# Routing with fewer TensorE transposes: every fourth tile's rows of the second half turned by VectorE and DMA, the last fold by halves of slots, two stores by halves

## The chip, the cores and the metric

The kernel runs on one core of a Trainium2 chip. A core has five engines that run side by side: TensorE (PE; its weight loads are shown apart as PEld), VectorE (DVE), ScalarE (ACT), GpSimd (POOL) and SyncE (SP), which here issues transfers; 16 DMA engines carry them. The metric is the time of one launch in microseconds (us). Before the change it was 578.08 us, the median of three runs (577.79 to 578.09). In code P is 128, the partitions.

## The reference, cut to what matters

Four batches of 2048 tokens of 256 numbers go through a layer of linear attention and then a soft mixture of experts; all numbers are float32. The change touches the second part alone, where N is 64 tiles of 128 tokens here (the 16 experts with 16 slots give 256 columns):

```python
x = layernorm(x + attention(x))                       # not touched
xn = layernorm(x) * gamma + beta
logits = einsum('bnd,des->bnes', l2norm(xn) * scale, l2norm(mu))
dispatch = softmax(logits, axis=tokens)               # over the tokens of a batch
combine = softmax(logits, axis=(experts, slots))
slot_in = einsum('bnd,bnes->besd', xn, dispatch)      # the "fold"
h = gelu(einsum('besd,edh->besh', slot_in, w1) + b1)
slot_out = einsum('besh,ehd->besd', h, w2) + b2
out = layernorm(x + einsum('besd,bnes->bnd', slot_out, combine))   # the "mix"
```

## The kernel before, in words

The second part has three stages. **Routing** goes over 64 tiles of 128 tokens, four batches of TB = 16 tiles; four tiles (GT) are a group, and there are 16 groups (GROUPS), group k with its tokens in buffer q = k % 4. For each group GpSimd adds beta to the scaled tokens (`add_beta`), TensorE turns the rows by eight transposes, four tiles by two halves of the 256 numbers (`turn_xn`, L257), ScalarE rounds the turned tokens from the accumulator banks to xnT_hi (`round_xnT`, L264), and VectorE subtracts to get the rest xnT_lo (`split_xnT`, L269). For each tile TensorE then makes the logits with six matmuls (L1736 to L1738, hi and lo parts), ScalarE the exponentials e_tok (L1634), and TensorE folds the tokens with them: two float32 matmuls, one for each half of the 256 slots (L1748; a float32 matmul appears in the trace as two). Logits run two tiles ahead of the fold (`LEAD`). VectorE turns each tile's exponentials in blocks of 32x32 (L1853), SyncE moves the blocks to their place with four transfers for each group (`exchange_e`, L1477), and from group 4 on it spills the tokens of a group to memory (`spill_x1`, L1487). VectorE also scales the tokens of group k+3 (L222), and GpSimd inverts the norms (L249) and makes ET_lo (L1542).

**Slots**: VectorE normalises the folded slots (`normalise_slots`, L1907 and L1909), TensorE turns them (L1776), multiplies by w1 and w2 (L1793, L1805) with ScalarE's gelu between, VectorE adds the bias in 16 pieces (L1944), and TensorE turns the outputs back with 16 transposes (L1814), four for each batch; ScalarE copies them out of the banks (L1694), VectorE makes three rests (L1953).

**Mix**: for each group TensorE multiplies (L1841 for groups 0 to 3, L1837 to L1839 for the rest), VectorE adds the tokens (L1963) and takes statistics (L1976), GpSimd and ScalarE help (L1588, L1702) and ScalarE normalises (L1709). SyncE reloads spilled tokens (L1501) and stores each finished group of 512 KB (L1520). The last group goes out in two halves, one issued by ScalarE (L1722) and one by SyncE (L1522).

The order on each engine is written out by hand, and semaphores tie the engines together. What waits where, around the change: the logits of a group's first tile wait for `xnT_split`; the exponentials of a tile wait for the turn of the tile four before (`e_turned`); a group's first turn of exponentials waits until the transfers of the group two before have landed (`e_moved`); SyncE issues strictly in its order.

Of the kernel before, what the change touches and what calls it, by code (L numbers as in the profile page):

```python
# [21 lines left out]
P = 128  # L22
# [7 lines left out]
def build(nc, x, xT, W1q, b1q, W2qT_b, W1k, b1k, W2kT_b, W1v, b1v, W2v, b2v, ln_w, ln_b,  # L30
# [21 lines left out]
    with top:  # L52
# [207 lines left out]

        def round_xnT(act, k, q):
            act.wait_ge(xnT_done, k + 1)
            for kb in range(KB):
                nc.scalar.copy(xnT_hi[q % 2][:, kb, :], xnT_ps[kb][:, :]).then_inc(xnT_rounded, 1)  # L264

        def split_xnT(dve, k, q, halves=range(KB)):
            for kb in halves:
                dve.wait_ge(xnT_rounded, KB * k + kb + 1)
                nc.vector.tensor_tensor(xnT_lo[q % 2][:, kb, :], xnT_ps[kb][:, :],  # L269
                                        xnT_hi[q % 2][:, kb, :].bitcast(F32), ALU.subtract).then_inc(xnT_split, 1)  # L270


        with ExitStack() as attn:
# [1077 lines left out]
        with ExitStack() as moe:  # L1351
# [3 lines left out]
            def msem(name):  # L1355
                return sem(name, moe)
# [9 lines left out]
            xnT_hi.append(msb("xnT_hi1", [P, KB, GTOK], F32R))  # L1366
            xnT_lo.append(msb("xnT_lo1", [P, KB, GTOK], F32R))
            e_tok = msb("e_tok", [P, 4, ES])
            e_turn = [msb(f"e_turn{i}", [P, FOUR, SB, GT, QUAD]) for i in range(2)]
            SPLIT = (1, 2, 3)  # L1370
            FIRST = GB * SPLIT[0]
# [90 lines left out]
            last_stored = [msem(f"last_stored{pair}") for pair in range(2)]  # L1462

            block = moe.enter_context(nc.Block())

            @block.sync
            def _(sp):
                for kb in range(KB):
                    sp.dma_start(w1_sb[:, kb, :, :], w1[:, kb * P:(kb + 1) * P, :].rearrange("e p h -> p e h")
                                 ).then_inc(w1_loaded, 16)  # L1470

                def exchange_e(g):

                    sp.wait_ge(e_turned, GT * g + 2 * GT)
                    for j in range(FOUR):
                        quad = slice(QUAD * j, QUAD * j + QUAD)
                        sp.dma_start(ET_all[:, g, :, quad],  # L1477
                                     e_turn[g % 2][quad, :, :, :, :].rearrange("r f s t c -> r (f s t c)")
                                     ).then_inc(e_moved[g % 2], 16)

                def spill_x1(g):

                    sp.wait_ge(tok_scaled, GT * g)
                    n = g - FIRST
                    if n > 1:
                        sp.wait_ge(x1_spilled[n % 2], 16 * (n // 2))
# [25 lines left out]
                for g in range(FIRST, AGAIN):  # L1512
                    reload_x1(g)
                for k in range(LAST):
                    if k + AGAIN in SPLIT_GROUPS:
                        reload_x1(k + AGAIN)
                    sp.wait_ge(y_normed, GT * k + GT)
                    if k >= GB:
                        sp.wait_ge(stored[k % GB], 16 * (k // GB))
                    sp.dma_start(out_t[:, GT * k:GT * k + GT, :], y[k]).then_inc(stored[k % GB], 16)  # L1520
# [3 lines left out]
                for pair in range(2):  # L1524
                    sp.wait_ge(last_stored[pair], 16)
                for q in range(GB):
                    sp.wait_ge(stored[q], 16 * (B - 1 if q == LAST % GB else B))

            @block.gpsimd
            def _(pool):  # L1530
# [14 lines left out]
                def route(b, last):  # L1545
                    for q in range(GB):
                        if not (last and q == GB - 1):
                            if b == 0 and q == 1:
                                invert_o(pool, GROUPS - 1, 1)
                            if b > 0 or q > 0:  # L1550
                                invert_norms(pool, GB * b + q + 1, (q + 1) % GB, minus_half[:, :])
                        if not (last and q >= GB - 3):
                            add_beta(pool, GB * b + q + 3, (q + 3) % GB)
                        if GB * b + q - 2 in SPLIT_GROUPS and not (last and q == GB - 1):
# [73 lines left out]
            def _(act):  # L1628
# [97 lines left out]
            def _(pe):  # L1726
                def logits(b, t):
                    q = t // GT % GB
                    toks = slice((t % GT) * P, (t % GT + 1) * P)
                    if t % GT == 0:  # L1730
                        pe.wait_ge(xnT_split, KB * (GB * b + t // GT + 1))
                    pe.wait_ge(e_ready, TB * b + t + 1)
                    ps = log_ps[t % 2][:, 0:ES]
                    for kb in range(KB):
# [6 lines left out]
                def fold(b, t):  # L1741
# [3 lines left out]
                    if t == 0 and b > 1:  # L1745
                        pe.wait_ge(slot_inT_ready, SB * b)
                    for s in range(SB):
                        last = nc.tensor.matmul(fold_ps(b)[s][:, 0:D + 1], e_tok[:, t % 4, s * P:(s + 1) * P],  # L1748
                                                xn[q][:, t % GT, :], start=(t == 0), stop=(t == TB - 1))
                        if b == B - 1 and t == TB - 1 and s == 0:  # L1750
                            last.then_inc(half_folded, 1)
                    last.then_inc(tile_folded, 1)

                def lead(b, t, last):
                    logits(b, t)
                    k, q = GB * b + t // GT + 1, (t // GT + 1) % GB
                    if t % GT == 1 and not (last and q == 0):
                        turn_xn(pe, k, q)

                def route(b, last):  # L1760
                    for t in range(TB):
                        if t < TB - 1 and not (last and t + LEAD >= TB):
                            lead(b, t + LEAD, last)
                        fold(b, t)
                        if t == 1 and b > 0:
                            turn_slots(b - 1)
# [33 lines left out]
                for half in range(2):  # L1800
                    pe.wait_ge(hs_ready, half + 1)
                    for db in range(KB):
# [3 lines left out]
                                                    w2_sb[:, r, db * P:(db + 1) * P], hs[:, r, :],  # L1806
                                                    start=True, stop=True)
                        last.then_inc(soT_done, 1)
                for n in range(B):
                    pe.wait_ge(soT_ready, 3 * B + n + 1)  # L1810
                    for s in range(SB):
                        for db in range(KB):
                            at = s * D + db * P
                            last = nc.tensor.transpose(so_ps[n][:, at:at + P],  # L1814
                                                       soT[:, db, n, s * P:(s + 1) * P], ident[:, :])
                    last.then_inc(so_done, 1)
# [29 lines left out]
            def _(dve):  # L1846
# [10 lines left out]
                def route(b, last):  # L1857
                    a, p = GROUPS - 1, 1
                    for t in range(TB):
# [28 lines left out]
                        if b == 1 and t == 10:  # L1888
                            shift_z(dve, a, p)
                        if t % GT == 1 and not (last and q == GB - 1) and not (b == 0 and q == 0):  # L1890
                            split_xnT(dve, k + 1, (q + 1) % GB)
# [158 lines left out]
```

## Time and profile before

| what | value |
|---|---|
| median of 3 runs | 578.08 us |
| the profiled execution's own time | 578.1 us |
| its span | 576.4 us |
| PE busy | 564.3 us (98% of the span) |
| DVE, ACT, POOL busy | 84%, 71%, 74% |
| granted TensorE clock, mean | 0.995 of full speed |
| DMA | 59.66 MB, 166932 packets, of them 139854 under 512 B |

The profiled execution lies 1.7 us above its span and agrees with the median. Busy time of an engine is counted from the records of its instructions; for PE the ends of matmuls are modelled, so that records overlap, and what a matmul costs in a full queue is the distance to the start of the next one. In the second part, routing runs from 394 to 509 us of the span, the slots to 520, the mix to 568, and the rest until 576.4 is the end of the last groups and their stores.

### The profile page before, as it was taken

Reading aid. Unit: us, or ns where it says so; the run is one execution under the profiler, and the core shown is the slowest. Engines: PE = TensorE matmul, PEld = TensorE weight load, DVE = VectorE, ACT = ScalarE, POOL = GpSimd, SP = SyncE. Lnnn points to the kernel's source line nnn. Section 1 sums busy time; section 2 is a strip of 40 time slices with the busy share of each in tenths; the row PEclk is TensorE's granted clock in tenths of the full one; section 3 lists DMA queues with packets and bytes.
Section 4 is the critical chain, followed back from the end, with each engine's and each line's share of the span. In section 5 each row is a group of like instructions: output and inputs, shape, how many; then the busy total and the mean of one; then the engine's idle time right before and its main releaser. Section 6 shows DMA issues by size and latency. Waiting matters only on the chain. (4 is left out here: it accounts for less than half of the span.)

```text
span 576.4 us, 12092 instructions
## 1 busy us (share of the span) xinstructions
PE 564.3 (98%) x3892; PEld 525.8 (91%) x3892; DVE 486.1 (84%) x1037; ACT 406.7 (71%) x870; POOL 425.7 (74%) x437
## 2 busy tenths in 40 slices
PE   8999999999999999999999999999999999999994
PEld 7999989999899999999999999998999999988994
DVE  6579889799898889988889889988989777557996
ACT  4775666676767667667576766677679988754886
POOL 0779879788797887977979779795667777643664
PEclk9999999999999999999999999999999999999997
DMA  8424134042240422413224133023777777784986
GB/s 219 102 75 110 24 88 91 21 111 34 77 109 6 104 31 78 109 15 94 38 72 109 18 91 73 3 38 74 148 151 146 146 147 145 130 136 136 327 295 220
DMA packets 166932, 59.66 MB, mean 104 GB/s; under 512 B 139854, under 2 KB 159724, under 8 KB 166892
## 3 DMA queue, kind: packets, MB, share of 16 engines
q1 hardware_dynamic: 166608, 58.89, 43.9%
q8 instruction: 21, 0.34, 0.2%
q10 hardware_dynamic: 284, 0.27, 0.1%
q14 instruction: 19, 0.16, 0.1%
HBM read 27.68 MB, written 14.68 MB: 74 GB/s over the span
## 5 line engine op out<-in xcount | busy, mean ns | idle before, releaser
L529 POOL TENSOR_TENSOR h_lo<-xn_all,h_hi 128x512 fp32r<-128x512 f32 x32 | 41.3, 1291 | 63.3 <-ACT xn_all L648 62.2
L646 ACT ACTIVATE h_hi<-bank,bias_col 128x512 fp32r<-128x512 f32 x96 | 66.4, 692 | 18.5 <-PE bank L806 16.8
L804 PE MATMUL bank<-xnT_hi,w_hi 128*128 128x512 f32 x188 | 76.2, 405 | 0.0
L805 PE MATMUL bank<-xnT_lo,w_hi 128*128 128x512 f32 x188 | 74.4, 396 | 0.0
L806 PE MATMUL bank<-xnT_hi,w_lo 128*128 128x512 f32 x188 | 74.2, 395 | 0.0
L681 ACT CAST state_hi<-bank 128x512 fp32r<-128x512 f32 x57 | 33.6, 589 | 48.6 <-PE bank L939 48.6
L1748 PE MATMUL bank<-xn_all,e_tok 128*128 128x257 f32 x256 | 65.1, 379 | 0.0
L1207 DVE TENSOR_TENSOR state_lo<-bank,state_hi 128x512 fp32r<-128x512 f32 x57 | 39.4, 692 | 28.3 <-ACT state_hi L681 28.2
L1853 DVE STREAM_TRANSPOSE e_turn<-e_tok 128x256 f32<-128x256 f32 x64 | 40.2, 637 | 16.1 <-ACT e_tok L1634 15.0
L1634 ACT ACTIVATE e_tok<-bank,shift,xinv 128x256 f32<-128x256 f32 x64 | 36.1, 564 | 19.1 <-PE bank L1738 12.3
L1748 PEld LDWEIGHTS bank<-xn_all,e_tok 128*128 128x128 f32 x256 | 44.1, 189 | 3.8
L1736 PE MATMUL bank<-mu_hi,xnT_hi 128*128 128x256 f32 x128 | 46.9, 366 | 0.5 <-POOL blank L1534 0.5
L672 ACT CAST v_hi<-xn_all 128x512 fp32r<-128x512 f32 x32 | 19.9, 622 | 34.4 <-DVE xn_all L1162 34.3
L547 POOL TENSOR_TENSOR vsum_lo<-v_sum,vsum_hi 128x512 fp32r<-128x512 f32 x32 | 41.2, 1289 | 3.5 <-ACT vsum_hi L667 3.5
L806 PEld LDWEIGHTS bank<-xnT_hi,w_lo 128*128 128x128 f32 x188 | 35.4, 188 | 8.7
L541 POOL TENSOR_TENSOR v_lo<-xn_all,v_hi 128x512 fp32r<-128x512 f32 x32 | 42.9, 1362 | 0.0
L535 POOL TENSOR_TENSOR ktok_lo<-xn_all,ktok_hi 128x512 fp32r<-128x512 f32 x32 | 38.2, 1196 | 6.0 <-ACT ktok_hi L662 6.0
L232 POOL TENSOR_TENSOR xn_all<-xn_all,b_rows 128x1024 f32<-128x1024 f32 x16 | 35.3, 2206 | 9.4 <-DVE xn_all L222 9.4
L805 PEld LDWEIGHTS bank<-xnT_lo,w_hi 128*128 128x128 f32 x188 | 35.4, 188 | 5.8
L804 PEld LDWEIGHTS bank<-xnT_hi,w_hi 128*128 128x128 f32 x188 | 35.5, 189 | 5.7
L524 POOL TENSOR_TENSOR x_all<-x_all,lnb_rows 128x512 f32 (+1 forms) x31 | 39.5, 1298 | 0.0
L515 POOL TENSOR_TENSOR xnT_lo<-xn_all,xnT_hi 128x512 fp32r<-128x512 f32 x30 | 38.1, 1295 | 0.0
(228 smaller groups left out, 2202.4 us busy)
## 6 DMA issues: line engine op xcount, KB each, us to landing
x_all<-in_L_attn_x SPq DMA_DIRECT2D x16, 512.0 KB, 3.9
kT<-k_turn SPq DMA_DIRECT2D x128, 64.0 KB, 2.5
ET_all<-e_turn SPq DMA_DIRECT2D x64, 128.0 KB, 4.0
xn_all<-in_xT SPq DMA_DIRECT2D x15, 512.0 KB, 4.6
x_spill<-x_all SPq DMA_DIRECT2D x12, 512.0 KB, 3.2
ET_all<-x_spill SPq DMA_DIRECT2D x8, 512.0 KB, 5.6
out<-ET_all SPq DMA_DIRECT2D x7, 512.0 KB, 2.9
out<-x_all SPq DMA_DIRECT2D x4, 512.0 KB, 4.4
```

What stands on the lines that cost most here:

```text
L524: pool.tensor_tensor(xp, xp, lnb_rows[:, :].unsqueeze(1).to_broadcast([P, 2, D]), ALU.add).then_inc(xb_ready, 1)
L529: pool.tensor_tensor(h_lo[:, V_SLOT, m, :], hv[:, m, :], h_hi[:, V_SLOT, m, :].bitcast(F32), ALU.subtract).then_inc(hv_split, 1)
L541: pool.tensor_tensor(v_lo[:, pair, :], v_tok[:, pair, :], v_hi[:, pair, :].bitcast(F32), ALU.subtract).then_inc(v_split, 1)
L547: pool.tensor_tensor(vsum_lo[:, pair, :], v_sum[:, pair, :], vsum_hi[:, pair, :].bitcast(F32), ALU.subtract).then_inc(vsum_split, 1)
L646: nc.scalar.activation(h_hi[:, h_slot(j, n), m, :], ps, ACT.Gelu, bias=bias(n, m))
L804: nc.tensor.matmul(ps, w[0], xs[0], start=start, stop=False, skip_group_check=shared)
L805: nc.tensor.matmul(ps, w[0], xs[1], start=False, stop=False, skip_group_check=shared)
L806: return nc.tensor.matmul(ps, w[1], xs[0], start=False, stop=stop, skip_group_check=shared)
L1207: nc.vector.tensor_tensor(lo[:, :, :], state_halves, hi[:, :, :].bitcast(F32), ALU.subtract).then_inc(state_split, 1)
L1736: nc.tensor.matmul(ps, hi, mu_hi[:, kb, :], start=(kb == 0), stop=False)
L1748: last = nc.tensor.matmul(fold_ps(b)[s][:, 0:D + 1], e_tok[:, t % 4, s * P:(s + 1) * P], xn[q][:, t % GT, :], start=(t == 0), stop=(t == T ...
L1853: nc.vector.transpose(e_turn[q % 2][:, :, :, t % GT, :], e_tok[:, t % 4, :].rearrange("p (s r f) -> p f s r", s=SB, f=FOUR)).then_inc(e_tu ...
```

## The change

1. For groups 8 to 15 (`TURNED`) TensorE turns three tiles of four. The fourth, 128 tokens by 256, is turned by VectorE in blocks of 32x32 (`turn_side`, two groups ahead), moved by four transfers (`exchange_side`), rounded by ScalarE and split by GpSimd (`split_side`). ScalarE's roundings and VectorE's splits from the banks get a quarter smaller. The logits of the fourth tile wait for the new `side_split`.
2. In the last batch the folds of tiles 14 and 15 are issued slots 0 to 127 of both first, then slots 128 to 255 of both (`fold_last`).
3. The turning back of the expert outputs is issued half by half for the first two batches.
4. Groups 13 and 14 are stored in halves of 256 KB, each as soon as its two tiles are normalised.

In the diff, `exchange_side` and `store_halves` are SyncE's, `split_side` is GpSimd's and is called behind `invert_norms(k)`, `turn_side` is VectorE's.

```diff
-        def turn_xn(pe, k, q):
+        def turn_xn(pe, k, q, tiles=GT):
...
-                for t in range(GT):
+                for t in range(tiles):
...
+            TURNED = range(2 * GB, GROUPS)
+            x_turn = msb("x_turn", [P, 2, FOUR, KB, QUAD])
+            x_side = msb("x_side", [P, 2, KB, P])
...
+                def exchange_side(k):
+                    n = k - TURNED[0]
+                    sp.wait_ge(side_turned, n + 1)
+                    if n > 1:
+                        sp.wait_ge(side_split, n - 1)
+                    for j in range(FOUR):
+                        quad = slice(QUAD * j, QUAD * j + QUAD)
+                        sp.dma_start(x_side[:, n % 2, :, quad],
+                                     x_turn[quad, n % 2, :, :, :].rearrange("r f k c -> r (f k c)")
+                                     ).then_inc(side_moved[n % 2], 16)
...
+                    if g + 2 in TURNED:
+                        exchange_side(g + 2)
                     if g + GB - 1 in SPLIT_GROUPS:
                         spill_x1(g + GB - 1)
                     exchange_e(g)
...
+                def store_halves(k):
+                    for half in range(2):
+                        tiles = slice(2 * half, 2 * half + 2)
+                        sp.wait_ge(y_normed, GT * k + 2 * half + 2)
+                        sp.dma_start(out_t[:, GT * k + 2 * half:GT * k + 2 * half + 2, :], y[k][:, tiles, :]
+                                     ).then_inc(half_stored[half] if k < LAST - 1 else last_stored[2 + half], 16)
...
+                def split_side(k):
+                    n = k - TURNED[0]
+                    pool.wait_ge(side_rounded, n + 1)
+                    pool.tensor_tensor(xnT_lo[k % 2][:, :, SIDE], x_side[:, n % 2, :, :],
+                                       xnT_hi[k % 2][:, :, SIDE].bitcast(F32), ALU.subtract).then_inc(side_split, 1)
...
                         if t % GT == 1:
-                            round_xnT(act, k, q)
+                            if k in TURNED:
+                                round_xnT(act, k, q, slice(0, (GT - 1) * P))
+                                n = k - TURNED[0]
+                                act.wait_ge(side_moved[n % 2], 16 * FOUR * (n // 2 + 1))
+                                nc.scalar.copy(xnT_hi[q % 2][:, :, SIDE], x_side[:, n % 2, :, :]
+                                               ).then_inc(side_rounded, 1)
+                            else:
+                                round_xnT(act, k, q)
...
+                    if t % GT == GT - 1 and GB * b + t // GT in TURNED:
+                        pe.wait_ge(side_split, GB * b + t // GT - TURNED[0] + 1)
...
+                def fold_last(b, tiles):
+                    for s in range(SB):
+                        for t in tiles:
+                            if s == 0:
+                                pe.wait_ge(e_ready, TB * b + t + 3)
+                            last = fold_half(b, t, s)
+                            if s == SB - 1:
+                                last.then_inc(tile_folded, 1)
+                        if s == 0:
                             last.then_inc(half_folded, 1)
...
-                for n in range(B):
-                    pe.wait_ge(soT_ready, 3 * B + n + 1)
-                    for s in range(SB):
...
+                for n in range(B // 2):
+                    turn_outputs(n, 0)
+                for n in range(B // 2):
+                    turn_outputs(n, 1)
+                for n in range(B // 2, B):
+                    turn_outputs(n, 0)
+                    turn_outputs(n, 1)
...
+                        if t % GT == 1 and k + 2 in TURNED:
+                            turn_side(k + 2)
...
+                def turn_side(k):
+                    n = k - TURNED[0]
+                    dve.wait_ge(xn_ready, k + 1)
+                    if n > 1:
+                        dve.wait_ge(side_moved[n % 2], 16 * FOUR * (n // 2))
+                    nc.vector.transpose(x_turn[:, n % 2, :, :, :],
+                                        xn[k % GB][:, GT - 1, 0:D].rearrange("p (k r f) -> p f k r", k=KB, f=FOUR)
+                                        ).then_inc(side_turned, 1)
```

On SyncE, in the second half of routing, the order of transfers was this (ET_all<-e_turn are the turned exponentials, x_spill the spilled tokens):

```order
L1487 DMA x_spill<-x_all 128x1024
L1477 DMA ET_all<-e_turn 128x8x32 x4
L1487 DMA x_spill<-x_all 128x1024
L1477 DMA ET_all<-e_turn 128x8x32 x8
L1510 DMA xn_all<-in_L_ffn_w 64x8x256 x2
```

and is now this (x_side<-x_turn is the turned fourth tile):

```order
L1519 DMA x_side<-x_turn 128x2x32 x4
L1496 DMA x_spill<-x_all 128x1024
L1486 DMA ET_all<-e_turn 128x8x32 x4
L1519 DMA x_side<-x_turn 128x2x32 x4
L1486 DMA ET_all<-e_turn 128x8x32 x4
L1532 DMA xn_all<-in_L_ffn_w 64x8x256 x2
```

The four new transfers of a group stand between the exchange of the group before and the spill.

On VectorE, around the first group of batch 3 (colinv and slot_in normalise the slots of the batch before, xnT_lo is the split, n_low the floor of the norms, xn_all<-x_all the scaling of a later group), before:

```order
L1911 RECIPROCAL rinv<-rsum 128x16
L1853 STREAM_TRANSPOSE e_turn<-e_tok 128x8x32 x2
L269 TENSOR_TENSOR xnT_lo<-bank,xnT_hi 128x512 x2
L1853 STREAM_TRANSPOSE e_turn<-e_tok 128x8x32
L244 TENSOR_SCALAR n_low<-n 128x4
```

and now:

```order
L1999 RECIPROCAL rinv<-rsum 128x16
L1929 STREAM_TRANSPOSE e_turn<-e_tok 128x8x32 x2
L269 TENSOR_TENSOR xnT_lo<-bank,xnT_hi 128x384 x2
L1983 STREAM_TRANSPOSE x_turn<-xn_all 128x256
L1929 STREAM_TRANSPOSE e_turn<-e_tok 128x8x32
L244 TENSOR_SCALAR n_low<-n 128x4
```

The new turn stands behind the split and ahead of the third turn of exponentials and the floor of the norms.

On TensorE, from the last folds to the turning back of the outputs (bank6 and bank7 take the two halves of the slots, and later the outputs of batches 0 and 1), before:

```order
L1748 MATMUL bank6<-xn_all,e_tok 128x257
L1748 MATMUL bank7<-xn_all,e_tok 128x257
L1776 MATMUL bank6<-ident,slot_in 128x128 x2
L1776 MATMUL bank7<-ident,slot_in 128x128 x2
...
L1814 MATMUL bank6<-ident,slot_inT 128x128 x4
L1814 MATMUL bank7<-ident,slot_inT 128x128 x4
L1814 MATMUL bank2<-ident,slot_inT 128x128 x4
L1814 MATMUL bank3<-ident,slot_inT 128x128 x4
```

and now:

```order
L1803 MATMUL bank6<-xn_all,e_tok 128x257 x2
L1803 MATMUL bank7<-xn_all,e_tok 128x257 x2
L1844 MATMUL bank6<-ident,slot_in 128x128 x2
L1844 MATMUL bank7<-ident,slot_in 128x128 x2
...
L1881 MATMUL bank6<-ident,slot_inT 128x128 x2
L1881 MATMUL bank7<-ident,slot_inT 128x128 x2
L1881 MATMUL bank6<-ident,slot_inT 128x128 x2
L1881 MATMUL bank7<-ident,slot_inT 128x128 x2
L1881 MATMUL bank2<-ident,slot_inT 128x128 x4
L1881 MATMUL bank3<-ident,slot_inT 128x128 x4
```

The second half of tile 14's fold has moved behind the first half of tile 15's, and four of the sixteen output transposes stand ahead of the ones that need the second half of the bias additions.

## Rows read from the trace of the kernel before

**Rows 1.** Busy time by stretch: PE, PEld, DVE, ACT, POOL; granted clock, DMA share, GB/s.

```profile
452.00:480.00 28.00, 28.00 (x193) 26.36 (x192) 22.44 (x49) 24.48 (x77) 21.67 (x13) 1.00 0.73 144
480.00:508.60 28.60, 28.60 (x188) 26.70 (x187) 17.24 (x35) 22.60 (x69) 16.93 (x9) 1.00 0.80 143
550.00:568.20 18.20, 18.20 (x154) 17.99 (x152) 17.40 (x40) 16.32 (x33) 12.52 (x26) 1.00 0.70 247
```

**Rows 2.** Who waited for whom, 452 to 506: total us, times, longest.

```profile
POOL xinv L249 <- DVE n_low L244: 10.7, 7, 3.3
ACT e_tok L1634 <- PE bank L1738: 6.5, 11, 1.0
```

**Rows 3.** TensorE, one group's transposes and what follows: start, us, what.

```profile
473.92 1.04 PE L257 MATMUL bank<-ident,xn_all 128*128 128x128 f32 x8
474.80 1.03 PE L1748 MATMUL bank<-xn_all,e_tok 128*128 128x257 f32 x4
```

**Rows 4.** The engines in order of time, 451 to 459.

```profile
451.21 4.24 SPq L1477 DMA_DIRECT2D ET_all<-e_turn  x4
453.88 1.07 ACT L264 CAST xnT_hi<-bank 128x512 fp32r<-128x512 f32 x2 [0.22 <-PE bank L257]
454.67 1.24 DVE L269 TENSOR_TENSOR xnT_lo<-bank,xnT_hi 128x512 fp32r<-128x512 f32 x2
457.19 0.36 PE L1736 MATMUL bank<-mu_hi,xnT_hi 128*128 128x256 f32 x1
458.12 0.33 SPq L1487 DMA_DIRECT2D x_spill<-x_all  x1
458.94 0.66 DVE L1853 STREAM_TRANSPOSE e_turn<-e_tok 128x256 f32<-128x256 f32 x1 [0.30 <-ACT e_tok L1634]
```

**Rows 5.** Transfers: count, size of one, median us to landing (first 452 to 480, then whole span).

```profile
ET_all<-e_turn SPq DMA_DIRECT2D x15, 128.0 KB, 4.0
kT<-k_turn SPq DMA_DIRECT2D x128, 64.0 KB, 2.5
```

**Rows 6.** Two single microseconds; the last two columns are DMA share and GB/s.

```profile
457.00:458.00 1.00, 1.00 (x11) 1.00 (x10) 1.00 (x3) 0.79 (x1) 0.78 (x1) 1.00 0.60 89
458.00:459.00 1.00, 1.00 (x8) 0.89 (x7) 0.70 (x3) 0.82 (x3) 0.83 (x1) 1.00 0.13 45
```

**Rows 7.** From the last folds to the mix, by engine: start, us, what.

```profile
506.24 2.77 PE L1748 MATMUL bank<-xn_all,e_tok 128*128 128x257 f32 x12
508.61 0.17 DVE L1907 RECIPROCAL colinv<-bank 128x1 f32<-128x1 f32 x1 [0.84 <-PE bank L1748]
509.41 0.48 DVE L1909 TENSOR_SCALAR slot_in<-bank,colinv 128x256 f32<-128x256 f32 x1
509.83 0.37 ACT L1674 COPY slot_inT<-bank 128x256 f32<-128x256 f32 x1 [1.22 <-PE bank L1776]
518.28 1.97 PE L1814 MATMUL bank<-ident,slot_inT 128*128 128x128 f32 x16 [0.38 <-DVE slot_inT L1944]
518.98 0.59 ACT L1694 COPY w_sb<-bank 128x512 f32<-128x512 f32 x1 [2.31 <-PE bank L1814]
519.98 6.13 PEld L1841 LDWEIGHTS bank<-w_sb,ET_all 128*128 128x128 f32 x29
524.36 0.64 POOL L1588 TENSOR_TENSOR x_all<-xn_all,x_all 128x256 f32<-128x256 f32 x1 [4.70 <-ACT xn_all L1702]
```

**Rows 8.** The last stores: issues, DMA share, and size and median us to landing.

```profile
572.40 0.37 SPq L1522 DMA_DIRECT2D out<-ET_all  x1
571.50:572.00 0.50, 0.00 (x0) 0.00 (x0) 0.36 (x2) 0.00 (x0) 0.10 (x1) 0.50 0.46 150
575.00:575.50 0.50, 0.00 (x0) 0.00 (x0) 0.00 (x0) 0.00 (x0) 0.00 (x0) 0.50 0.85 303
out<-ET_all SPq DMA_DIRECT2D x3, 512.0 KB, 2.9
out<-ET_all SPq DMA_DIRECT2D x1, 256.0 KB, 3.5
```

More of the change, by code:

```diff
@@ L259, in turn_xn, with round_xnT, split_xnT @@
             last.then_inc(xnT_done, 1)
-        def round_xnT(act, k, q):
+        def round_xnT(act, k, q, toks=slice(0, GTOK)):
             act.wait_ge(xnT_done, k + 1)
             for kb in range(KB):
-                nc.scalar.copy(xnT_hi[q % 2][:, kb, :], xnT_ps[kb][:, :]).then_inc(xnT_rounded, 1)
-        def split_xnT(dve, k, q, halves=range(KB)):
+                nc.scalar.copy(xnT_hi[q % 2][:, kb, toks], xnT_ps[kb][:, toks]).then_inc(xnT_rounded, 1)
+        def split_xnT(dve, k, q, halves=range(KB), toks=slice(0, GTOK)):
             for kb in halves:
                 dve.wait_ge(xnT_rounded, KB * k + kb + 1)
-                nc.vector.tensor_tensor(xnT_lo[q % 2][:, kb, :], xnT_ps[kb][:, :],
-                                        xnT_hi[q % 2][:, kb, :].bitcast(F32), ALU.subtract).then_inc(xnT_split, 1)
+                nc.vector.tensor_tensor(xnT_lo[q % 2][:, kb, toks], xnT_ps[kb][:, toks],
+                                        xnT_hi[q % 2][:, kb, toks].bitcast(F32), ALU.subtract).then_inc(xnT_split, 1)
         with ExitStack() as attn:
@@ L1368, in build @@
             e_tok = msb("e_tok", [P, 4, ES])
+            TURNED = range(2 * GB, GROUPS)
+            x_turn = msb("x_turn", [P, 2, FOUR, KB, QUAD])
+            x_side = msb("x_side", [P, 2, KB, P])
+            side_turned = msem("side_turned")
+            side_moved = [msem(f"side_moved{i}") for i in range(2)]
+            side_rounded = msem("side_rounded")
+            side_split = msem("side_split")
+            SIDE = slice((GT - 1) * P, GT * P)
             e_turn = [msb(f"e_turn{i}", [P, FOUR, SB, GT, QUAD]) for i in range(2)]
@@ L1461, in build @@
             last_normed = msem("last_normed")
-            last_stored = [msem(f"last_stored{pair}") for pair in range(2)]
+            last_stored = [msem(f"last_stored{part}") for part in range(4)]
+            half_stored = [msem(f"half_stored{half}") for half in range(2)]
             block = moe.enter_context(nc.Block())
@@ L1516, in _ @@
                         reload_x1(k + AGAIN)
-                    sp.wait_ge(y_normed, GT * k + GT)
                     if k >= GB:
                         sp.wait_ge(stored[k % GB], 16 * (k // GB))
+                    if k >= LAST - 2:
+                        store_halves(k)
+                        continue
+                    sp.wait_ge(y_normed, GT * k + GT)
                     sp.dma_start(out_t[:, GT * k:GT * k + GT, :], y[k]).then_inc(stored[k % GB], 16)
@@ L1523, in _ @@
                              ).then_inc(last_stored[1], 16)
-                for pair in range(2):
-                    sp.wait_ge(last_stored[pair], 16)
+                for part in range(4):
+                    sp.wait_ge(last_stored[part], 16)
+                for half in range(2):
+                    sp.wait_ge(half_stored[half], 16)
                 for q in range(GB):
-                    sp.wait_ge(stored[q], 16 * (B - 1 if q == LAST % GB else B))
+                    sp.wait_ge(stored[q], 16 * len(range(q, LAST - 2, GB)))
             @block.gpsimd
@@ L1551, in route @@
                                 invert_norms(pool, GB * b + q + 1, (q + 1) % GB, minus_half[:, :])
+                            if GB * b + q + 1 in TURNED:
+                                split_side(GB * b + q + 1)
                         if not (last and q >= GB - 3):
@@ L1747, in fold, with fold_half @@
                     for s in range(SB):
-                        last = nc.tensor.matmul(fold_ps(b)[s][:, 0:D + 1], e_tok[:, t % 4, s * P:(s + 1) * P],
-                                                xn[q][:, t % GT, :], start=(t == 0), stop=(t == TB - 1))
-                        if b == B - 1 and t == TB - 1 and s == 0:
+                        last = fold_half(b, t, s)
+                    last.then_inc(tile_folded, 1)
+                def fold_half(b, t, s):
+                    return nc.tensor.matmul(fold_ps(b)[s][:, 0:D + 1], e_tok[:, t % 4, s * P:(s + 1) * P],
+                                            xn[t // GT][:, t % GT, :], start=(t == 0), stop=(t == TB - 1))
+                def fold_last(b, tiles):
[3 more added lines that the diff above has]
+                                pe.wait_ge(e_ready, TB * b + t + 3)
+                            last = fold_half(b, t, s)
+                            if s == SB - 1:
+                                last.then_inc(tile_folded, 1)
+                        if s == 0:
                             last.then_inc(half_folded, 1)
-                    last.then_inc(tile_folded, 1)
                 def lead(b, t, last):
@@ L1757, in lead @@
                     if t % GT == 1 and not (last and q == 0):
-                        turn_xn(pe, k, q)
+                        turn_xn(pe, k, q, GT - 1 if k in TURNED else GT)
                 def route(b, last):
@@ L1763, in route @@
                             lead(b, t + LEAD, last)
+                        if last and t >= TB - LEAD:
+                            if t == TB - 1:
+                                fold_last(b, range(TB - LEAD, TB))
+                            continue
                         fold(b, t)
@@ L1808, in _, with turn_outputs @@
                         last.then_inc(soT_done, 1)
-                for n in range(B):
-                    pe.wait_ge(soT_ready, 3 * B + n + 1)
-                    for s in range(SB):
[L1812 to L1816, printed above, removed]
+                def turn_outputs(n, s):
+                    pe.wait_ge(soT_ready, (2 * s + 1) * B + n + 1)
+                    for db in range(KB):
+                        at = s * D + db * P
+                        last = nc.tensor.transpose(so_ps[n][:, at:at + P],
+                                                   soT[:, db, n, s * P:(s + 1) * P], ident[:, :])
+                    if s == SB - 1:
+                        last.then_inc(so_done, 1)
+                for n in range(B // 2):
[5 more added lines that the diff above has]
+                    turn_outputs(n, 1)
                 for moved in e_moved:
@@ L1890, in route @@
                         if t % GT == 1 and not (last and q == GB - 1) and not (b == 0 and q == 0):
-                            split_xnT(dve, k + 1, (q + 1) % GB)
+                            split_xnT(dve, k + 1, (q + 1) % GB, toks=slice(0, (GT - 1) * P)
+                                      if k + 1 in TURNED else slice(0, GTOK))
+                        if t % GT == 1 and k + 2 in TURNED:
+                            turn_side(k + 2)
                         if t % GT == 2 and not (last and q == GB - 1) and not (b == 0 and q == 0):
```

## The prediction

> **What bounds the kernel now.** I read the busy time by stretch first. In both batches that the change touches TensorE is busy for the whole stretch, 28.00 of 28.00 and 28.60 of 28.60 us, at the full granted clock, while VectorE stands at 22.4 and 17.2 and GpSimd at 21.7 and 16.9 [rows 1]. TensorE's records overlap, so I check it by the waits: ScalarE waited 11 times for logits, 6.5 us in all, GpSimd 7 times for the floor of the norms, 10.7 us, and TensorE appears in no row as one that waits [rows 2]. So routing runs at TensorE's rate, some 7.1 us a group (56.6 us for eight groups). The mix is the same: TensorE 18.20 of 18.20 us [rows 1]. So what TensorE starts earlier there arrives at the end. Only two stretches are otherwise: the slots, where the chain changes between VectorE and TensorE [rows 7], and the last microseconds, where the DMA engines are full [rows 8].
>
> **The transposes that go.** Eight groups lose two of eight transposes, 16 in all. Eight start at 473.92 and the fold behind them at 474.80 [rows 3], so one costs 0.88/8 = 0.11 us, and 16 cost 1.76 us. All stand in the full queue: gain 1.76.
>
> The row shows a transpose every 0.11 us. The Trainium skill ("TensorE: Matmul & The Clock Gate", Part 4) gives a 128x128 transpose in TensorE's transpose mode about 275 ns inside a kernel, mostly access latency. By that the 16 would give 4.4 us; the trace disagrees, since only the latency of a single one can be so long, not the pace of eight.
>
> **What replaces them**, for each of the eight groups:
> - VectorE turns one tile of 128x256 as it does for the exponentials, 0.66 us, and its two splits shrink by a quarter, 1.24/4 = 0.31 [rows 4]. Net +0.35, from 80% to 85% of its time. It stands behind the split, so the split, which TensorE waits for, comes no later; it ends at 455.91 and the logits that need it start at 457.19 [rows 4], 1.3 us of slack. Behind the new turn are queued the third turn of exponentials and the floor of the norms, then GpSimd's inversion, then ScalarE's exponentials of the next group's first tile. ScalarE waits for TensorE there, not the reverse, and logits run two tiles ahead, so I take 0. With that cover gone, it costs 0.35 x 8 = 2.8 us.
> - SyncE issues four transfers, 32 KB each. An issue that isn't held up takes 0.33 us [rows 4], four 1.3. The turn ends at about 455.9 - 0.3 + 0.65 = 456.3, the issues by 457.6, before the spill at 458.12, so nothing behind them is late. Were each held up like one of the exchange, 4.24/4 = 1.06 us, they would end at 460.5 and push spill and exchange by 2.4 us.
> - The DMA engines move a quarter of the exchange's bytes in pieces of the same shape (32 numbers), about 4.24/4 = 1.06 us of their time. They are free for 0.40 and 0.87 us in the two microseconds ahead of the spill's data [rows 6], which holds it. The share of a group goes from 0.73 x 7.1 = 5.2 us to 6.2 of 6.9. The exchange must have landed when VectorE begins the group after next: the last of four issued from 451.21 starts at about 454.5 and lands 4.0 later [rows 5], 458.5, and the turn at 458.94 waited for ScalarE alone [rows 4]. Slack 0.4 there, and 1.3 more before TensorE's logits wait. I take 0; ends 0 and 1.06 - 0.4 for each of seven groups, 4.6 us, if all passes through.
> - ScalarE's two roundings shrink by about 0.27 and a copy of 0.37 is added [rows 4, 7]: +0.1, nothing. It waits for the transfers first. It reaches that place at 453.88 + 7.1 + 0.8 = 461.8; the last transfer, issued at 457.3, lands at 459.8 by the 64 KB row (2.5) or 461.3 by the 128 KB row (4.0) [rows 5]. I take no wait, the smaller row being nearer to 32 KB.
> - GpSimd subtracts 128x256, 0.64 us [rows 7], against 10.7/7 = 1.5 us of waiting in each group [rows 2]. TensorE needs it only for the group's fourth tile, over 6 us after ScalarE's copy. Nothing.
>
> The exchange of the exponentials moves 89 GB/s at a share of 0.60, where large pieces move 303 at 0.85 [rows 6, 8]. The Trainium skill ("DMA: Bandwidth & Descriptors", Specifications) asks for 512 B or more in a piece for the full rate; 128 B pieces are on the wrong side, and the trace agrees. This rule speaks against the change; its price is the 1.06 us above.
>
> **The last fold.** Six folds, 12 records, start at 506.24 and take 2.77 us [rows 7], 0.43 for a half fold at the usual pace. VectorE's first reciprocal started at 508.61, when the last tile's first half was done. Now that half ends one half fold earlier, at 508.15. VectorE finishes the first half at 508.85, then waits for all folds at 509.0, and needs 0.7 more: 509.71 instead of 509.89 (509.41 + 0.48) [rows 7]. TensorE's turn and all behind it gain 0.18. Ends 0.1 and 0.43.
>
> **The output transposes.** Sixteen start at 518.28 and the mix at 519.98 [rows 7], 0.106 each. Four move ahead of the wait for VectorE, into 0.38 us in which TensorE stood idle; they need 0.42. So the mix starts 0.42 - 0.04 = 0.38 earlier, if ScalarE's first copy permits: it began at 518.98 after four transposes [rows 7], now after two, at 518.77, and ends at 519.36, before 519.6. Gain 0.38, lower end the 0.21 of that copy. TensorE is full from there to 568.2, so it is kept.
>
> **The stores.** At the end 512 KB of group 14 and the last group's two pieces of 256 KB, the last issued at 572.40, share the engines, which are 0.46 busy at 571.5 and still 0.85 busy at 575 [rows 8]. At about 345 GB/s a half of group 14 is 0.75 us of data. It now goes two normalisations, 1.1 us, earlier, into the hole before 572.5. The last piece, issued at 572.40, landed 3.5 later [rows 8], at 575.9; one of 512 KB with free engines needs 2.9 [rows 8], 575.3. Gain 0.6; ends 0 and 0.75.
>
> **Sum**: 1.76 + 0.18 + 0.38 + 0.6 = 2.9 us. The profiled execution's span goes from 576.4 to 573.5; with the 1.7 us outside the span this is 575.2, and the profiled execution (578.1) agrees with the median, so 575.2 is the forecast, 0.5% below.
>
> **The rivals.**
> - *The covers hold only in part.* VectorE's 0.35 us for each group, or a late exchange, reaches TensorE. For it: the DMA engines at 90%, and slacks of 0.4 us on one path. Against it: 1.3 us more before TensorE waits. VectorE's 2.8 us in half the groups is 1.4: 576.6.
> - *The tail gives nothing.* The end is set by the last store's own latency, and copies of ScalarE and VectorE set the mix's start. Against it: the engines' full share until 575. Only 1.76 and 0.3 remain: 576.0.
> - *Slower: the transfer queue becomes the bound of routing.* If a transfer costs SyncE and the queues by its number and not by its bytes, four more are 4.24 us, and 5.2 + 4.2 = 9.4 us a group passes the 6.9 that TensorE needs. It decides from 1.7 us for the four. At 9.4, seven groups lose 2.3 each over today, 16 us: 578.1 + 16.1 - 1.2 = 593. At 2.3 us for the four the period is 7.5, seven groups lose 0.4 against today, and with 1.2 from the tail it is 578.1 + 2.8 - 1.2 = 579.7. For it: issues of the exchange take 1.06 each. Against it: the spill, four times larger than one of them, is issued in 0.33, so the cost goes with the pieces.
> - *A removed transpose is worth 0.27 us*, as a mechanism: each would then keep the array for its whole record of 0.27. The pace in rows 3 excludes it; it would give 575.2 - 2.6 = 572.6.
>
> **How the numbers follow.** Forecast 0.65, covers in part 0.15, tail without gain 0.13, slower 0.05, the 0.27 us 0.02. A measurement here tells 0.2% from no change, 1.16 us, so faster means below 576.9. The forecast, the tail case, most of the part case and the last are below: 0.65 + 0.13 + 0.06 + 0.02 = 0.86; within 0.2%: 0.10; slower: 0.04. The range runs from 574.5 (the upper ends of fold and stores, 0.4 more, and 0.3 of dropped waits) to 577.0, which takes in the tail case and most of the part case.
>
> **What would show it.** Right: in the second half a group takes 6.9 us instead of 7.1, TensorE busy in all of it, six transposes in a row; SyncE's new issues end before the spill, no wait of ScalarE for x_side over 0.5 us, no long wait of VectorE for ET_all; the mix starts 2.3 us earlier than 519.98, at 517.7; TensorE's end at 565.9; the engines full until about 572.5 rather than 575.4, the last landing less than 3.2 us after its issue. Wrong: TensorE waiting for xnT_lo or e_tok in batches 2 and 3, the four new transfers taking over 1.7 us, or a group of 7.1 us or more.

## The result: 1.05% slower, and the profile after

The changed kernel takes 584.17 us, median of 5 runs (583.20 to 584.83), against 578.09 us (577.79 to 578.21). The ratio is 1.0105, 95% interval 1.0095 to 1.0116: 6.1 us slower where 2.9 us faster was forecast.

The stretches that answer to [rows 1], changed kernel; columns PE, PEld, DVE, ACT, POOL, then clock, DMA share, GB/s:

```profile
452.00:480.00 28.00, 25.27 (x170) 23.17 (x169) 19.01 (x44) 21.54 (x73) 23.00 (x15) 1.00 0.72 136
480.00:508.60 28.60, 24.37 (x157) 21.71 (x156) 18.67 (x42) 20.67 (x72) 18.92 (x13) 1.00 0.71 135
```

TensorE, full before, now has holes of 2.7 and 4.2 us. The clock stayed at 1.00, and the DMA share did not rise. The waits between 452 and 506 (total, times, longest), to be held against [rows 2]:

```profile
DVE e_turn L1929 <- DMA ET_all<-e_turn: 15.1, 7, 3.5
ACT xnT_hi L1691 <- DMA x_side<-x_turn: 11.6, 6, 2.7
PEld bank L1787 <- DVE xnT_lo L269: 6.3, 4, 1.8
PE bank L1787 <- ACT e_tok L1676: 6.0, 5, 1.4
```

Read from the bottom: TensorE waits for VectorE's split and ScalarE's exponentials, and these two engines wait for transfers. So the next view is SyncE's own order (start, time for which it is held, what), which answers to [rows 4]:

```profile
454.31 0.55 SPq L1496 DMA_DIRECT2D x_spill<-x_all  x1
454.90 4.24 SPq L1486 DMA_DIRECT2D ET_all<-e_turn  x4
459.24 3.59 SPq L1519 DMA_DIRECT2D x_side<-x_turn  x4
462.93 0.55 SPq L1496 DMA_DIRECT2D x_spill<-x_all  x1
463.52 4.30 SPq L1486 DMA_DIRECT2D ET_all<-e_turn  x4
467.92 3.52 SPq L1519 DMA_DIRECT2D x_side<-x_turn  x4
```

SyncE has no pause: 459.24 to 462.83, 462.93 to 463.48, 463.52 to 467.82, 467.92. From spill to spill it takes 8.62 us here, and 8.43 on the mean of six rounds (446.20 to 496.80). The same six rounds took 7.28 each before the change, and TensorE would need 7.05 now (no_transfer, below). Before the change SyncE waited some 2.5 us a round for VectorE, in front of the spill (452 to 506, as [rows 2]):

```profile
SPq L1487 <- DVE xn_all L222: 12.4, 5, 2.8
```

The side transfers alone, after the change, by instruction (duration ns minimum/median/maximum; then us to landing):

```profile
L1519 SPq DMA_DIRECT2D x_side<-x_turn x32: 613/616/1823, 442.8 to 504.3; - x32
DMA to landing us min/median/max: 2.0/2.1/3.4
```

None held SyncE for under 0.61 us. The last two of each four took 0.61 each; the first two, right behind the exchange, took 1.7 to 2.4 us together. The landing itself is short. The damage on ScalarE, one group:

```profile
469.53 0.84 ACT L264 CAST xnT_hi<-bank 128x384 fp32r<-128x384 f32 x2
472.89 0.41 ACT L1691 CAST xnT_hi<-x_side 128x256 fp32r<-128x256 f32 x1 [2.52 <-DMA x_side<-x_turn]
474.00 0.36 PE L1787 MATMUL bank<-mu_hi,xnT_hi 128*128 128x256 f32 x1 [1.40 <-ACT e_tok L1676]
```

It stood 2.52 us in front of the side tile, with the exponentials of the third tile queued behind it, and TensorE ran dry for 1.40 us. The mix's first weight load, at 519.98 in [rows 7], comes at 526.85:

```profile
526.85 3.32 PEld L1917 LDWEIGHTS bank<-w_sb,ET_all 128*128 128x128 f32 x16 [0.76 <-issue]
```

So 6.9 us are lost up to there, where 2.3 were to be gained: 9.2 us off. After it 0.9 us is won (the span grew by 6.0).

The transposes did what was forecast. Six take the place of eight [rows 3], and 467.75 to 468.40 is 0.108 each:

```profile
467.75 0.81 PE L257 MATMUL bank<-ident,xn_all 128*128 128x128 f32 x6
468.40 1.03 PE L1803 MATMUL bank<-xn_all,e_tok 128*128 128x257 f32 x4
```

### The profile page after: what moved, and what is told of

The parts are those of the page before. It is cut to its first block and busy times, and to the rows that moved or that the text cites. A ratio compares the mean times of both kernels' runs of the same rounds, so it can differ in the third digit from the quotient of the medians.

```text
span 582.4 us, 12140 instructions
## 1 busy us (share of the span) xinstructions
PE 563.7 (97%) x3876; PEld 522.5 (90%) x3876; DVE 488.4 (84%) x1045; ACT 405.2 (70%) x878; POOL 433.4 (74%) x445
## 5 line engine op out<-in xcount | busy, mean ns | idle before, releaser
L529 POOL TENSOR_TENSOR h_lo<-xn_all,h_hi 128x512 fp32r<-128x512 f32 x32 | 41.4, 1294 | 63.0 <-ACT xn_all L648 61.9
L249 POOL TENSOR_TENSOR xinv<-n_low,minus_half 128x4 f32<-128x4 f32 x16 | 19.4, 1210 | 27.2 <-DVE n_low L244 27.2
L524 POOL TENSOR_TENSOR x_all<-x_all,lnb_rows 128x512 f32 (+1 forms) x31 | 39.6, 1304 | 0.0
```

Source lines behind the costliest of these rows:

```text
L524: pool.tensor_tensor(xp, xp, lnb_rows[:, :].unsqueeze(1).to_broadcast([P, 2, D]), ALU.add).then_inc(xb_ready, 1)
L529: pool.tensor_tensor(h_lo[:, V_SLOT, m, :], hv[:, m, :], h_hi[:, V_SLOT, m, :].bitcast(F32), ALU.subtract).then_inc(hv_split, 1)
```

## The experiments

Ten kernels were run. Ratios are to the kernel before on the same chip (its median 577.9, 577.9 and 577.6 us in the three sets), with 95% intervals. The theory: SyncE's queue is full in the second half of routing, since each of the small transfers holds it for at least 0.61 us however little it moves. Rivals: the pieces of 128 B on the DMA engines; the added work of VectorE, ScalarE and GpSimd; the halves of fold, transposes and stores.

**tail_only.** The halves alone.

```diff
-            TURNED = range(2 * GB, GROUPS)
+            TURNED = range(0)
```

> The changed kernel with no group turned aside (TURNED empty): only the last fold by halves, the output transposes by halves and the stores by halves stay. Theory (SyncE's queue is full in the second half of routing, and that alone makes the change slow): these three parts bring what was forecast, 1.2 us, so 576.9 us; the mix starts 0.56 us earlier than before. Rival (the halves are themselves part of the loss): 578 or more.

Measured: 576.50 us, ratio 0.9976 (0.9967 to 0.9985). The halves gain 1.4 us where 1.16 was forecast. Its rows answer to [rows 7, 8]:

```profile
508.23 0.17 DVE L1995 RECIPROCAL colinv<-bank 128x1 f32<-128x1 f32 x1 [0.41 <-PE bank L1803]
517.43 2.08 PE L1881 MATMUL bank<-ident,slot_inT 128*128 128x128 f32 x16
519.24 10.88 PEld L1917 LDWEIGHTS bank<-w_sb,ET_all 128*128 128x128 f32 x51
571.66 0.37 SPq L1554 DMA_DIRECT2D out<-ET_all  x1
573.50:574.00 0.50, 0.00 (x0) 0.00 (x0) 0.00 (x0) 0.00 (x0) 0.00 (x0) 0.50 0.86 307
574.00:574.90 0.90, 0.00 (x0) 0.00 (x0) 0.00 (x0) 0.00 (x0) 0.00 (x0) 0.50 0.01 1
```

The first reciprocal comes 0.38 earlier, the output transposes no longer stop for VectorE, and the mix starts 0.74 earlier (forecast 0.56). The last store goes out 0.74 earlier and its data end 1.4 us earlier, near 574.0 instead of past 575, so the stores gave 0.7 of it (forecast 0.6). The rival, that the halves share in the loss, falls.

**no_transfer.** All of the change but the transfers.

```diff
-                    if g + 2 in TURNED:
-                        exchange_side(g + 2)
...
-                                act.wait_ge(side_moved[n % 2], 16 * FOUR * (n // 2 + 1))
-                                nc.scalar.copy(xnT_hi[q % 2][:, :, SIDE], x_side[:, n % 2, :, :]
+                                act.wait_ge(side_turned, n + 1)
+                                nc.scalar.copy(xnT_hi[q % 2][:, :, SIDE], x_turn[:, n % 2, :, :, :]...
...
```

> The changed kernel with the four transfers of each side tile left out: ScalarE and GpSimd read the tile as VectorE turned it, so its blocks are not moved to their place. All other work of the change stays. Theory (SyncE's queue): all of the loss goes, and the forecast comes, 575.2 us. Rival (VectorE's turn, ScalarE's copy and GpSimd's subtraction, 0.93 us instead of 0.64, reach TensorE): 577 to 580. Both: the group's period says it, 6.9 us in the first, over 7.2 in the rival.

Measured: 574.64 us, ratio 0.9947 (0.9932 to 0.9963), 1.9 us under tail_only where the transposes were worth 1.76. TensorE is full again (columns as above), and the spills stand 6.91 us apart in these rows, 7.05 on the mean of six (443.48 to 485.81):

```profile
452.00:480.00 28.00, 28.00 (x188) 26.23 (x187) 23.23 (x54) 25.58 (x85) 26.73 (x17) 1.00 0.76 155
464.23 0.33 SPq L1496 DMA_DIRECT2D x_spill<-x_all  x1
471.14 0.33 SPq L1496 DMA_DIRECT2D x_spill<-x_all  x1
```

GpSimd's subtraction took 0.93 us in six of the eight groups, not 0.64, and stayed hidden. The transfers alone, then, cost 584.17 - 574.64 = 9.5 us (9.1 by the two ratios, which compare on one chip). That is the size of the whole error (584.17 - 575.2 = 9.0), and the rounds give it too: seven of 8.43 instead of 7.05 are 9.7 us.

**before_four.** The converse: the transfers alone, put into the kernel before.

```diff
+                    for j in range(4):
+                        quad = slice(QUAD * j, QUAD * j + QUAD)
+                        sp.dma_start(idle_to[:, :, quad],
+                                     idle_from[quad, :, :, :].rearrange("r f k c -> r (f k c)")).then_inc(idle_moved, 16)
...
                     if g + GB - 1 in SPLIT_GROUPS:
                         spill_x1(g + GB - 1)
```

The four also wait for the four before them and for a split of VectorE. Neither wait stops SyncE: from 442.25 to 504.94 no pause of it is over 0.05 us.

> The kernel before, with nothing of the change, plus four transfers of 32 KB in each of groups 6 to 13, of the same shape and at the same place in SyncE's order as the side tile's; they move a constant that nobody reads. Theory (SyncE's queue is full): the exchange 4.2, four of these 3.3 and the spill 0.55 us and gaps make a period of 8.3 to 8.6 us where TensorE needs 7.15, so 586 us (8 groups by 1.2, less what the first absorb). Rival (the loss needs the side tile's own dependences, ScalarE waiting for x_side): within 1 us of before, 578 to 579.

Measured: 584.22 us, ratio 1.0112 (1.0097 to 1.0127): 6.3 us slower, somewhat less than the 8 expected. SyncE's round is 8.42 us on the mean of six, as in the changed kernel (8.43), where it was 7.28. Nobody reads what they move, so the wait of ScalarE for x_side isn't needed for a loss. It enters through the exchange behind them:

```profile
459.51 3.16 SPq L1515 DMA_DIRECT2D idle_to<-idle_from  x4
462.77 0.55 SPq L1491 DMA_DIRECT2D x_spill<-x_all  x1
463.37 4.26 SPq L1481 DMA_DIRECT2D ET_all<-e_turn  x4
467.73 3.28 SPq L1515 DMA_DIRECT2D idle_to<-idle_from  x4
DVE e_turn L1872 <- DMA ET_all<-e_turn: 19.8, 6, 4.7
```

**quarter** and **one_issue**: number against pieces.

```diff
-                        sp.dma_start(x_side[:, n % 2, :, quad],
-                                     x_turn[quad, n % 2, :, :, :].rearrange("r f k c -> r (f k c)")
+                        part = slice(QUAD * j, QUAD * j + QUAD // 4)
+                        sp.dma_start(x_side[0:P // 4, n % 2, :, quad],
+                                     x_turn[part, n % 2, :, :, :].rearrange("r f k c -> r (f k c)")
```

> The changed kernel with four transfers a group as it has them, but each moves 8 of its 32 partitions, a quarter of the pieces of 128 B (the rest of the tile holds a constant). Theory A (a transfer holds SyncE at least 0.61 us whatever it moves): the period stays near 8.0 us and the time within 1.5 us of the changed kernel, 582.5 to 584.2. Theory B (the pieces' time on the DMA engines): three quarters of the loss go, about 577.5.

```diff
-                    for j in range(FOUR):
...
+                    sp.dma_start(x_side[:, n % 2, :, 0:QUAD],
+                                 x_turn[:, n % 2, :, :, :].rearrange("p f k c -> p (f k) c")).then_inc(side_moved[n % 2], 16)
```

> The changed kernel with one transfer a group in place of four, of the same 128 KB in the same 1024 pieces of 128 B (each piece stays on its partition, so the tile is not the turned one). Theory A (number of transfers): SyncE's time falls from 3.5 to 0.6 - 1.7 us a group, the period to about 6.9, 575.5 us. Theory B (pieces): no change against the changed kernel, 584.

Measured: quarter 582.89 us, ratio 1.0082 (1.0066 to 1.0097); one_issue 574.52 us, ratio 0.9942 (0.9927 to 0.9957). With a quarter of the pieces in four transfers nearly all of the loss stays; with all the pieces in one it is gone. Their transfers:

```profile
L1523 SPq DMA_DIRECT2D x_side<-x_turn x32: 697/724/1861, 442.2 to 504.4; - x32
```

```profile
L1517 SPq DMA_DIRECT2D x_side<-x_turn x8: 670/988/1230, 441.8 to 491.2; - x8
DMA to landing us min/median/max: 3.7/4.0/5.0
452.00:480.00 28.00, 28.00 (x189) 26.25 (x187) 23.07 (x53) 26.07 (x88) 26.67 (x17) 1.00 0.86 167
```

The first fence is quarter, the second one_issue. A transfer of a quarter of the pieces holds SyncE no shorter, and the round is 8.44 us, with the DMA engines only 0.62 busy from 452 to 480 (0.73 before the change). In one_issue they are 0.86 busy, against 0.76 in no_transfer, and TensorE is full with a round of 7.07: the DMA time of the added pieces was there, some 0.7 us a group by these shares (an estimate), and was hidden. Its one transfer has another form, since each piece stays on its partition, so the two runs that follow keep the form and change the sum.

**two_quads.** Two of the four.

```diff
-                    for j in range(FOUR):
+                    for j in range(2):
```

> The changed kernel with two of the four transfers of each side tile left out (the other half of the columns holds a constant). Theory: SyncE's period is 4.2 + 0.55 + 1.9 + gaps = 6.9 us, at the edge of TensorE's 6.9, so nearly the time without any transfers, 574.6 to 576. Rival (any transfer between exchange and spill costs in proportion): half of the loss, 579.4.

Measured: 574.73 us, ratio 0.9948 (0.9933 to 0.9962): no loss at all, against 9.5 us for four. It is a threshold, not a price for each:

```profile
463.33 1.80 SPq L1522 DMA_DIRECT2D x_side<-x_turn  x2
465.23 0.55 SPq L1497 DMA_DIRECT2D x_spill<-x_all  x1
465.82 4.30 SPq L1487 DMA_DIRECT2D ET_all<-e_turn  x4
470.23 1.67 SPq L1522 DMA_DIRECT2D x_side<-x_turn  x2
```

SyncE's round is 6.90 us here and 7.10 on the mean of six (443.89 to 486.48), against the 7.05 that TensorE needs. From 456 to 493 no pause of SyncE is over 0.05 us either: its work just fits.

**long_pieces.** The side's four transfers untouched, the exchange's pieces made long.

```diff
-                        sp.dma_start(ET_all[:, g, :, quad],
+                        sp.dma_start(ET_all[quad, g, :, :].rearrange("p i c -> p (i c)"),
```

> The changed kernel with the exchange of the exponentials in pieces of 4 KB instead of 128 B: four transfers of 128 KB a group as before, each partition's row stays on its partition, so ET_all doesn't hold the turned exponentials. The side tile's four transfers are unchanged. Theory (SyncE's time is the sum of its issues; the exchange's 1.06 us each come from its 1024 pieces waiting for the DMA engines): the exchange's issues fall to 0.33 - 0.61, SyncE's period to 2 + 3.3 + 0.55 = 5.9 us at most, under TensorE's 6.9, and the time is that without transfers, 574.6 to 575.5. Rival (the four small transfers do harm by themselves, whatever else the queue holds): 580 or more.

Measured: 574.76 us, ratio 0.9948 (0.9930 to 0.9965).

```profile
459.46 2.51 SPq L1486 DMA_DIRECT2D ET_all<-e_turn  x4
462.19 2.69 SPq L1519 DMA_DIRECT2D x_side<-x_turn  x4
464.98 0.55 SPq L1496 DMA_DIRECT2D x_spill<-x_all  x1
```

The exchange holds SyncE 2.51 us instead of 4.3 and the four side transfers do no harm. The round is 7.07 again. It is the sum on SyncE that counts, whoever fills it. The long pieces also relieve the DMA engines (0.62 busy) and land sooner, 3.0 us after their issue where the short ones took 4.1, so this run alone doesn't exclude the engines as the cause; quarter and one_issue do. Of the exchange's 4.2 us, 2.5 are what four issues of at least 0.6 take, and the rest is there only with the short pieces.

**pool_issue.** Another engine issues.

```diff
+                def exchange_side(k):
+                    n = k - TURNED[0]
+                    pool.wait_ge(side_turned, n + 1)
...
+                        pool.dma_start(x_side[:, n % 2, :, quad],
```

> The changed kernel with the side tile's four transfers issued by GpSimd instead of SyncE, all correct. Theory: SyncE's order is as in the kernel without transfers; if GpSimd issues four in under 1 us (it has 6.9 - 1.2 - 0.9 - 2.2 - 2.4 = 0.2 us free a group with ET_lo's splits) the time is 574.6 to 576; every us more that it needs appears as a longer group, at 1 us for each transfer 8 x 3.8 = 30 us more, over 600. I expect about 590. Rival (it is the order in one queue or the DMA engines, not the issuing engine): as the changed kernel, 584.

Measured: 600.65 us, ratio 1.0386 (1.0371 to 1.0401). Each transfer held GpSimd 0.72 us, and it has no such time:

```profile
464.54 0.90 POOL L1575 TENSOR_TENSOR xnT_lo<-x_side,xnT_hi 128x256 fp32r<-128x256 f32 x1
465.40 2.91 POOL L1568 DMA_DIRECT2D x_side<-x_turn  x4
468.33 2.19 POOL L232 TENSOR_TENSOR xn_all<-xn_all,b_rows 128x1024 f32<-128x1024 f32 x1
```

Its round is 10.2 us (465.40 to the next four at 475.62). I had guessed 590, with a formula beside it that gave over 600 at 1 us for each transfer. At the measured 0.72 the formula gives 596 (574.6 and eight times 2.9 - 0.2), so it was nearer than the guess and still short by 4.6; GpSimd also waits 0.8 us a round for the floor of the norms.

**alternate** and **alternate_six**: versions that keep the sum on SyncE under TensorE's time.

```diff
-            TURNED = range(2 * GB, GROUPS)
+            TURNED = range(2 * GB + 1, GROUPS, 2)
...
-                    n = k - TURNED[0]
+                    n = TURNED.index(k)
```

The first is alternate's; alternate_six has range(GB + 1, GROUPS, 2).

> The changed kernel with only groups 9, 11, 13 and 15 turned aside, all correct. Theory: over two groups SyncE needs 2 x 4.95 + 3.4 = 13.3 us, under TensorE's 14.0, so half of the transposes' gain comes on top of the halves alone (576.5): 575.6. Rival (each burst of four is late by itself, whatever the mean): one loss of about 1.2 us for each of the four, 580.

> The changed kernel with groups 5, 7, 9, 11, 13 and 15 turned aside, all correct. Theory: SyncE has the same 13.3 us for two groups under 14.0, so two more groups give 2 x 0.22 = 0.44 us over the version with four groups (575.58): 575.1. Rival (in batch 1 VectorE and ScalarE carry the attention's rest too, and the waits for the exchange that four groups already show reach TensorE there): 576 or more.

Measured: alternate 575.58 us, ratio 0.9966 (0.9955 to 0.9976), as computed and better than both kernels; alternate_six 579.29 us, ratio 1.0024 (1.0012 to 1.0036), a miss. Most of its loss lies in batch 1, where groups 5 and 7 came in (above alternate, below alternate_six, as [rows 1]):

```profile
423.00:452.00 29.00, 29.00 (x197) 27.22 (x196) 25.43 (x56) 26.11 (x83) 18.90 (x15) 1.00 0.73 143
```

```profile
423.00:452.00 29.00, 26.91 (x180) 24.52 (x179) 22.32 (x51) 23.83 (x80) 17.81 (x15) 1.00 0.72 145
DVE e_turn L1929 <- DMA ET_all<-e_turn: 20.3, 7, 3.7
423.76 4.30 SPq L1486 DMA_DIRECT2D ET_all<-e_turn  x4
428.16 0.82 SPq L1496 DMA_DIRECT2D x_spill<-x_all  x1
429.03 5.35 SPq L1486 DMA_DIRECT2D ET_all<-e_turn  x4
432.26 0.66 DVE L1929 STREAM_TRANSPOSE e_turn<-e_tok 128x256 f32<-128x256 f32 x1 [3.67 <-DMA ET_all<-e_turn]
```

From 400 to 510 VectorE waited 20.3 us for the exchange, against 4.2 in alternate. The trace shows where that begins: the turn at 432.26 waits 3.67 us for the exchange that was issued behind the first four side transfers, from 423.76 on. Its last transfer landed 5.2 us after its own issue, at 432.24. In alternate the same exchange starts at 422.23, its last transfer lands after 3.8 us at 429.10, and the turn follows at 429.37: that path has under 0.3 us of slack.

The sum on SyncE did not stay as computed either. It was put at 13.3 us for two groups in both. In alternate transfers held SyncE 11.7 to 12.2 us, in alternate_six 13.2 to 14.0. There two exchanges stand back to back, and the second holds SyncE longer (5.35 us at 429.03). So the hold of a transfer isn't a constant, and a mean under TensorE's time isn't the whole condition. Why that landing took 5.2 us, with the spill and the next exchange issued right behind it, isn't settled.

## Why the prediction was wrong

- *What bounds the kernel.* Right: TensorE's rate, and what is gained before the mix arrives at the end (no_transfer, two_quads).
- *The transposes, 1.76 us.* Right: 0.108 each, 1.9 us between tail_only and no_transfer.
- *VectorE, ScalarE, GpSimd at nothing.* Right as computing work: no_transfer loses nothing. GpSimd's piece was mis-sized, up to 0.93 for 0.64.
- *The DMA engines, 1.06 us hidden.* Right that it is hidden: one_issue. The 1.06 itself was a quarter of the 4.24 for which the exchange held SyncE, not a time measured on the DMA engines; by their shares it was about 0.7.
- *"SyncE issues four transfers ... An issue that isn't held up takes 0.33 us [rows 4], four 1.3 ... so nothing behind them is late."* This step failed. The 0.33 was read from the spill, a transfer of another form. The like rows were in the same trace: the exchange's fastest issue and kT<-k_turn, half as large as one of the exchange, both have a minimum of 0.609 us. Four took 3.1 to 3.8 us. And SyncE's own time was never summed. Before the change 4.24 + 0.33 and gaps are 4.8 us of a round of 7.28, so 2.5 us were free, and 2.3 of the 7.05 wanted now. Four transfers need more, two (1.7 to 2.5 us) just fit. The exchange thus came late in every round, and VectorE and ScalarE with it. The other end, "were each held up like one of the exchange", gave 2.4 us late, and was not carried into the sum of a group.
- *ScalarE's wait.* It was costed by the landing (measured 2.1 us, even less than the 2.5 taken), not by when the fourth issue comes.
- *The rivals.* The slower rival had the mechanism, a queue that charges by the number, and a decision point of 1.7 us for the four. It added the four to the DMA engines' 5.2 us, not to SyncE's 4.8, and got 9.4 a group instead of the measured 8.4, and 593 instead of 584.2. Its chance, 0.05, was far too low: what I held against it, the spill's 0.33, was the same misread row. The prediction's signs of being wrong all came: TensorE waited for xnT_lo and e_tok, the four took over 1.7 us, and a group over 7.1.
- *The halves, 1.16 us.* Right in kind, 1.4 measured: fold and output transposes 0.74 for 0.56, the stores 0.7 for 0.6.

## What to carry to other kernels

An engine that issues transfers is an engine with a busy time of its own: add up how long each transfer holds it, by the row of the most similar form and not by the fastest one, and compare the sum with the period of the bound. Here two more transfers under that period were free, and four above it cost every group the difference. The sum is needed and not enough: alternate_six was under the period by its sum and lost, and its back-to-back exchanges held the queue longer and landed later. Splitting a small move into four cost four issues, however little each moved (quarter).

## What the runs showed of the hardware that wasn't expected

- A transfer across partitions in pieces of 128 B held SyncE 0.61 us at the least with 32, 64 or 128 KB, and 0.70 when it moved a quarter of 32 KB. A plain one of 512 KB held it 0.33, 0.55 right behind the small ones, and up to 1.05 in one_issue. GpSimd was held 0.72 by the same small transfer.
- The four transfers of an exchange held SyncE 4.2 us in pieces of 128 B and 2.5 in pieces of 4 KB, with the same bytes.
- GpSimd's subtraction of 128x256 into a rounded type took 0.93 us in six groups and 0.73 in the last two, where its sum of 128x256 in float32 takes 0.64 [rows 7]. The type alone doesn't explain it: at 128x512 both take 1.29 to 1.30 (before the change, L529 and L524). The cause is open.
